# A graph attention kernel: three small products go from VectorE to GpSimd, weighted values one body later, score transposes to the middle of TensorE's body

## The chip, the cores and the metric

One core of a Trainium2 chip runs the whole program. The metric is the device time of one execution in microseconds, lower is better; the median of several executions is quoted. Five engines work side by side, each with its own instruction stream, and meet in semaphores: TensorE (PE), VectorE (DVE), ScalarE (ACT), GpSimd (POOL) and SyncE (SP, which only issues DMAs here).

## The reference, cut to what matters

A graph has N=6250 nodes and E=200000 edges, each edge with 128 features, a source `src` and a destination `dst`; the edges are sorted by `dst`. There are H=8 heads of D=16 values.

```python
ke = layer_norm(einsum('ef,hfd->hed', x_edge, Wke), gke, bke)   # ve likewise
rel_k = layer_norm(concatenate([ke, k[:, src]], -1) @ relk_W + relk_b, relk_g, relk_beta)
qk = sum(q[:, dst] * rel_k, -1) / 4.0                            # one score per edge and head
lse = log(segment_sum(exp(qk - m[dst]), dst)) + m                # m: maximum per node
rel_v = layer_norm(concatenate([ve, v[:, src]], -1) @ relv_W + relv_b, relv_g, relv_beta)
h = (qk - lse[dst])[..., None] * rel_v
agg = segment_sum(h, dst)
z = layer_norm(relu(agg @ z_W + z_b), z_g, z_beta)
x = layernorm(x + z)
```

Since `lse` is not known while the edges are walked, the kernel sums both `rel_v` and `qk * rel_v` per node and combines them at the end.

## The kernel before, in words

The program has three parts: `start` makes node tables and index data (some 200 us), `edges` walks the edges, and `tail` forms the log-sum-exp, combines the sums and writes the output (from about 2890 us on). The change touches `edges` alone.

**Tiling.** An edge group is 512 edges, four tiles of 128 (`GE`, `TILES`); there are `GROUPS` = 391. A batch is 3 groups. Every engine runs the same software pipeline: in its body `c` it does stage after stage, each on another group `x = c - lag`, so a body of an engine handles one group in each stage. `every` (L1001) writes 24 bodies out, puts 12 bodies in a hardware loop and writes the last ones out. The order of the stages in a body is written by hand, and so are the semaphore waits: each buffer is a ring indexed by `x` modulo its depth, and a stage waits for its inputs and for its ring slot to be free.

**A group's way** (in brackets the lag):
- SP loads the edge features (L1048, [0]), every third body the codes and the gather columns (L1064, L1065), the query rows (L1074, [1]), stores the sums (L1079, [12]) and every third body the transposed scores (L1091).
- PE transposes the features into the PSUM bank `eat_ps` (L1142, [0]); ACT copies them (L1213). PE projects them twice (`project`, L1120): for the layer norm's squares ([1]) and for the values ([3]). ACT squares (L1228), DVE reduces (L1420, [2]), ACT takes logarithm and exponential (L1235, L1249), DVE scales the values into `p` (L1402, [4]).
- POOL gathers the source nodes' rows by four indirect DMAs, one a tile (L1298, [3]), into a ring of three; it waits for the columns and for DVE's add of three groups before.
- DVE adds the rows to `p` (L1350, [5]). ACT squares it into `z` (L1221, [5]). PE makes 0/1 matrices from the codes (L1135 [4] and L1160 [5], both in the bank `misc`, copied by ACT in L1207 and L1242) and expands the queries (L1167, [5]). DVE multiplies queries by keys (L1367, [6]) and reduces squares and products to `zs` (L1385, [6]); ACT makes 1/norm for keys, `zr` (L1265, [7]), and for values, `zw` (L1266, [7]).
- Three DVE operations of 32 columns per partition follow, all [8]: the score's main part `qk0 = zs*zr` (L1358), the score `hh[.., 1, C] = qk0 + z[.., C]` (L1376), and the weight `zw[.., 1] = score * zw[.., 0]` (L1393). L1410 ([8]) multiplies the values by both weights into `hh`.
- PE sums `hh` by destination in two halves (`sums`, L1113, [9]), ACT copies each half (L1198).
- At a batch's end PE transposes its scores from `hh` into the bank `misc`, at the very end of the body (L1186, [9]), and ACT copies them at the end of its body (L1273). The next use of `misc` is L1135, at the start of PE's next body, which waits for that copy (`s_qktc`, L1134).

DVE's order in a body is L1350, L1358, L1367, L1376, L1385, L1393, L1402, L1410, L1420. PE's is L1135, L1142, first half of the sums, first projection, L1160, L1167, second half, second projection, L1186.

Of the kernel before, what the change touches and what calls it, by code (L numbers as in the profile page):

```python
# [5 lines left out]
P = 128  # L6
N, E, F, H, D = 6250, 200000, 128, 8, 16
C = D - 1
HC = H * C
TILES = 4  # L10
# [22 lines left out]
BATCH = 3  # L33
# [906 lines left out]
def edges(nc, a, t):  # L940
# [5 lines left out]
    EA, QR, RR, PR, HR, OR, AG, ZR = 4, 6, 3, 6, 6, 6, 4, 3  # L946
# [12 lines left out]
    zs = sb("e_zs", [P, 2, TILES, 3 * H])  # L959
    zln = sb("e_zln", [P, TILES, 2 * H])  # L960
    zr = sb("e_zr", [P, 2, TILES, H])
    zw = sb("e_zw", [P, 2, TILES, H, 2])
# [68 lines left out]
    with nc.Block(no_gpsimd_drain=True) as block:  # L1031
# [69 lines left out]
        def _(pe):  # L1101
# [22 lines left out]
            def body(c, i, loop):  # L1124
                x = c - 4
                if is_group(x, loop):
# [18 lines left out]
                x = c - 1  # L1145
                if is_group(x, loop):
# [4 lines left out]
                    project(x, i, 0, y_ps, s_y)  # L1151
                x = c - 5
                if is_group(x, loop):
                    n, k, kb = UNROLL * i + x, x % QR, (x // BATCH) % FB
                    pe.wait_ge(s_oht, n + 2 if loop or x < GROUPS - 1 else n + 1)
                    if not loop and x == GROUPS - 1:
                        pe.wait_ge(s_qktc, (x - 5 - (BATCH - 1)) // BATCH + 1)
# [12 lines left out]
                sums(c - 9, i, loop, 1)  # L1170
# [6 lines left out]
                x = c - 9  # L1177
                if is_batch_end(x, loop):
                    n, ng = UNROLL * i + x, groups_in(x, loop)
                    x0 = x - (ng - 1)  # L1180
                    pe.wait_ge(s_oh, n + 5 if loop or x + 5 <= GROUPS else GROUPS)
                    if loop or x >= BATCH:
                        pe.wait_ge(s_qktc, batch(x, i))
                    h0 = x0 % HR
                    src = hh[:, h0:h0 + ng, :, :, 1, C].rearrange("p g t h -> p (g t h)")
                    nc.tensor.transpose(misc[0:H * TILES * ng, 0:P], src, ident[:]).then_inc(s_qkt, 1)  # L1186
            every(pe, body, GROUPS + 9)

        @block.scalar
        def _(act):  # L1190
# [9 lines left out]
            def body(c, i, loop):  # L1200
# [13 lines left out]
                copy_sums(c - 9, i, loop, 0)  # L1214
# [22 lines left out]
                if is_group(x, loop):  # L1237
# [4 lines left out]
                    nc.scalar.activation(oh[:, x % OR, :, :].rearrange("p j n -> p (j n)"), misc, ACT.Relu).then_inc(s_oh, 1)  # L1242
                x = c - 3
# [7 lines left out]
                if is_group(x, loop):  # L1251
# [4 lines left out]
                    nc.scalar.activation(zln[:], zs[:, x % 2, :, 0:2 * H], ACT.Ln, bias=t["eps_c"][:, 0:1], scale=1.0 / D).then_inc(s_zl, 1)  # L1256
                copy_sums(c - 9, i, loop, 1)
                x = c - 7
                if is_group(x, loop):
                    n = UNROLL * i + x  # L1260
                    act.wait_ge(s_zl, n + 1)
                    if loop or x >= 2:
                        act.wait_ge(s_qk0, n - 1)
                        act.wait_ge(s_h, n - 1)
                    nc.scalar.activation(zr[:, x % 2, :, :], zln[:, :, 0:2 * H:2], ACT.Exp, scale=-0.5).then_inc(s_zr, 1)  # L1265
                    nc.scalar.activation(zw[:, x % 2, :, :, 0], zln[:, :, 1:2 * H:2], ACT.Exp, scale=-0.5).then_inc(s_zw, 1)  # L1266
                x = c - 9
                if is_batch_end(x, loop):
                    b, kb, ng = batch(x, i), (x // BATCH) % 2, groups_in(x, loop)
                    act.wait_ge(s_qkt, b + 1)  # L1270
                    if loop or x // BATCH >= 2:
                        act.wait_ge(s_qst[kb], 16 * (2 * i + (x // BATCH) // 2))
                    nc.scalar.activation(qkt[0:H * TILES * ng, kb, :], misc[0:H * TILES * ng, 0:P], ACT.Copy).then_inc(s_qktc, 1)  # L1273
            every(act, body, GROUPS + 9)

        @block.gpsimd
        def _(pool):
# [10 lines left out]
            def body(c, i, loop):  # L1288
                x = c - 3
                if is_group(x, loop):  # L1290
                    n, k, kb = UNROLL * i + x, x % RR, (x // BATCH) % FB
                    pool.wait_ge(s_ft[kb], 32 * (i + (x // BATCH) // FB + 1))
                    if loop or x >= RR:
                        pool.wait_ge(s_pt, n - RR + 1)
                    pool.reg_add(last_node, nodes_less_2, 1)
                    for j in range(TILES):
# [4 lines left out]
            every(pool, body, GROUPS + 3)  # L1301

        @block.vector
        def _(dve):
# [39 lines left out]
            def body(c, i, loop):  # L1344
# [7 lines left out]
                x = c - 8  # L1352
                if is_group(x, loop):
                    n = UNROLL * i + x
                    dve.wait_ge(s_zr, n + 1)
                    if loop or x >= 1:
                        dve.wait_ge(s_qk, n)
                    v.tensor_tensor(out=qk0[:], in0=zs[:, x % 2, :, 2 * H:3 * H], in1=zr[:, x % 2, :, 0:H], op=ALU.mult).then_inc(s_qk0, 1)  # L1358
# [10 lines left out]
                x = c - 8  # L1369
                if is_group(x, loop):  # L1370
                    n = UNROLL * i + x
                    dve.wait_ge(s_qk0, n + 1)
                    if loop or x >= HR:
                        dve.wait_ge(s_agg, 2 * (n - HR) + 2)
                        dve.wait_ge(s_qkt, batch(x - HR, i) + 1)
# [730 lines left out]
```

## Time and profile before

| | |
|---|---|
| median of 3 runs (lowest to highest) | 3233.97 us (3225.24 to 3234.28) |
| the profiled execution | 3227.16 us, span 3225.4 us |
| busy: DVE / PE / POOL / ACT | 93% / 89% / 77% / 72% of the span |
| DMA traffic | 722.70 MB, mean 224 GB/s |
| mean granted TensorE clock | 0.962, full in the loop |

The profile is of one execution. A row of the order of time gives start, duration (both us), engine, source line, operation, output <- input, the shapes, the count, and in square brackets how long the engine had been idle before and which engine's work ended that. Consecutive DVE operations overlap in the record: a duration holds about 0.08 us that run beside the next start, so the step from start to start is the cost in line. GpSimd's rows leave out the register instructions and waits between two DMAs.

### The profile page before, as it was taken

The page shows a single profiled execution, that of the slowest core. Times are in us where ns is not written, and L with a number is a line of the kernel's source. Part 1 is how long each engine was busy: PE and PEld are TensorE (multiplying, and loading weights), DVE is VectorE, ACT ScalarE, POOL GpSimd, SP SyncE. Part 2 cuts the span into 40 slices and gives each one's busy share as a digit, 9 for nine tenths or more (in the row PEclk, how much of TensorE's full clock was granted, in tenths as well). Part 3 has the DMA queues.
Part 4 walks back from the last instruction along what each step waited for, and adds up shares of the span by engine and source line. Part 5 has one row for each costly group of instructions (what it writes and reads, how often), then busy time and mean ns, then how long its engine had stood idle before and what let it go on. Part 6 is the DMA issues. An engine that isn't in the chain of part 4 may idle for free. (4 is left out here: it accounts for less than half of the span.)

```text
span 3225.4 us, 74832 instructions
## 1 busy us (share of the span) xinstructions
PE 2876.7 (89%) x18674; PEld 2508.7 (78%) x18870; DVE 3004.0 (93%) x4143; ACT 2333.4 (72%) x5276; POOL 2472.7 (77%) x1853
## 2 busy tenths in 40 slices
PE   4659999999999999999999999999999999975734
PEld 3348888888888888888888888888888888863523
DVE  7879999999999999999999999999999999975645
ACT  2448877888887888878888877888878788752425
POOL 6678888888888888888888888888888888843871
PEclk9889999999999999999999999999999999997966
DMA  4567888888888888888888888888888888856521
GB/s 90 153 178 236 251 251 248 248 246 249 249 250 248 248 246 250 249 251 249 247 246 249 249 250 248 248 246 250 249 248 249 246 248 249 256 187 144 168 54 42
DMA packets 660641, 722.70 MB, mean 224 GB/s; under 512 B 97970, under 2 KB 554279, under 8 KB 659934
## 3 DMA queue, kind: packets, MB, share of 16 engines
q1 hardware_dynamic: 568057, 505.84, 49.4%
q0 software_dynamic: 84896, 211.67, 25.0%
q10 hardware_dynamic: 7620, 4.43, 0.6%
q8 instruction: 25, 0.41, 0.0%
q14 instruction: 43, 0.34, 0.0%
HBM read 482.87 MB, written 237.97 MB: 223 GB/s over the span
## 5 line engine op out<-in xcount | busy, mean ns | idle before, releaser
L1298 POOL DMA_INDIRECT e_rows<-node_table,e_gcol x1564 | 2181.0, 1395 | 479.0 <-issue 476.9
L1120 PE MATMUL banks<-w_edge,e_eat 128*128 128x240 f32 x6256 | 1399.2, 367 | 3.2 <-DVE e_p L1402 2.6
L1120 PEld LDWEIGHTS banks<-w_edge,e_eat 128*128 128x128 f32 x6256 | 1179.6, 190 | 115.4 <-DVE e_p L1402 11.3
L1113 PE MATMUL banks<-e_h,e_oh 128*128 128x256 f32 x3128 | 826.2, 387 | 8.2 <-ACT e_agg L1198 4.2
L1385 DVE TENSOR_REDUCE e_zs<-e_z 128x96 f32<-128x1440 f32 x391 | 646.2, 1653 | 0.2
L1113 PEld LDWEIGHTS banks<-e_h,e_oh 128*128 128x128 f32 x3128 | 533.5, 190 | 52.2 <-DVE e_h L1410 5.1
L1198 ACT ACTIVATE e_agg<-banks 128x512 f32<-128x512 f32 x782 | 465.4, 595 | 104.2 <-PE banks L1113 103.9
L1402 DVE TENSOR_TENSOR e_p<-banks,e_yr 128x960 f32<-128x960 f32 x391 | 449.1, 1149 | 3.4 <-PE banks L1120 3.4
L1410 DVE TENSOR_TENSOR e_h<-e_p,e_zw 128x960 f32<-128x960 f32 x391 | 449.3, 1149 | 0.1
L1350 DVE TENSOR_TENSOR e_p<-e_p,e_rows 128x960 f32<-128x960 f32 x391 | 449.3, 1149 | 0.0
L1420 DVE TENSOR_REDUCE e_yvar<-e_ysq 128x64 f32<-128x960 f32 x391 | 448.3, 1147 | 0.0
L1207 ACT ACTIVATE e_oht<-banks 128x512 bf16<-128x512 f32 x391 | 233.5, 597 | 282.6 <-remote 143.2
L1228 ACT ACTIVATE e_ysq<-banks 128x960 f32<-128x960 f32 x391 | 379.8, 971 | 50.4 <-PE banks L1120 6.7
L1221 ACT ACTIVATE e_z<-e_p 128x960 f32<-128x960 f32 x391 | 390.1, 998 | 0.0
L1167 PE MATMUL banks<-e_q,e_oht 128*128 128x128 bf16 x4692 | 325.8, 219 | 1.3 <-DVE e_z L1367 1.3
L1142 PE MATMUL banks<-ident,e_ea 128*128 128x128 f32 x1564 | 236.8, 274 | 77.5 <-ACT e_qkt L1273 43.1
L1167 PEld LDWEIGHTS banks<-e_q,e_oht 128*128 128x128 bf16 x4692 | 278.3, 98 | 1.7 <-issue 1.6
L1367 DVE TENSOR_TENSOR e_z<-e_p,banks 128x512 f32<-128x512 f32 x391 | 266.2, 681 | 0.0
L1142 PEld LDWEIGHTS banks<-ident,e_ea 128*128 128x128 f32 x1564 | 193.1, 141 | 80.3 <-DMA e_ea<-in_edge_attr 29.1
L1213 ACT ACTIVATE e_eat<-banks 128x512 f32<-128x512 f32 x391 | 231.2, 591 | 22.7 <-PE banks L1142 22.6
L1242 ACT ACTIVATE e_oh<-banks 128x512 f32<-128x512 f32 x391 | 229.6, 587 | 0.0
L1160 PEld LDWEIGHTS banks<-rank_code,e_feat 128*128 128x128 bf16 x1564 | 120.0, 98 | 46.1 <-ACT e_oht L1207 0.5
(412 smaller groups left out, 2570.6 us busy)
## 6 DMA issues: line engine op xcount, KB each, us to landing
tile_sums<-e_agg SPq DMA_DIRECT2D x391, 512.0 KB
e_q<-q_by_rank SPq DMA_DIRECT2D x1564, 96.0 KB
e_ea<-in_edge_attr SPq DMA_DIRECT2D x390, 256.0 KB
e_rows<-node_table,e_gcol POOLq DMA_INDIRECT x1564
edge_lse<-t_lse_sb SPq DMA_DIRECT2D x14, 448.0 KB, 3.6
edge_qk<-e_qkt SPq DMA_DIRECT2D x130, 48.0 KB
node_table<-n_tb SPq DMA_DIRECT2D x24, 240.0 KB, 2.6
t_x<-edge_qk SPq DMA_DIRECT2D x2, 2240.0 KB
```

Source lines behind the costliest of these rows:

```text
L1113: last = nc.tensor.matmul(agg_ps[:, (j % 2) * AW:(j % 2 + 1) * AW], oh[:, x % OR, j, :], hh[:, x % HR, j, :, :, :].rearrange("p h s d -> p ...
L1120: last = nc.tensor.matmul(out_ps[:, j // 2, (j % 2) * 2 * HC:(j % 2 + 1) * 2 * HC], eat[:, x % 4, j * P:(j + 1) * P], t["w_edge"][:, at:at ...
L1142: last = nc.tensor.transpose(eat_ps[:, j * P:(j + 1) * P], ea[:, k, j, :], ident[:])
L1167: last = nc.tensor.matmul(qx_ps[:, j * F:(j + 1) * F], oht[:, x % 2, j * P:(j + 1) * P], qw[:, k, j, part * F:(part + 1) * F], start=(part ...
L1198: nc.scalar.activation(agg[:, k, 2 * half:2 * half + 2, :].rearrange("p j c -> p (j c)"), agg_ps, ACT.Copy).then_inc(s_ags, 1)
L1221: nc.scalar.activation(z[:, x % ZR, :, 0:2 * H, 0:C], p[:, k, :, :, :, 0:C].rearrange("p t h k c -> p t (h k) c"), ACT.Square).then_inc(s_ ...
L1298: g.indirect_dma_start(out=rows[:, k, j, :], out_offset=None, in_=table, in_offset=bass.IndirectOffsetOnAxis(ap=gcol[:, kb, at:at + 1].bit ...
L1350: v.tensor_tensor(out=p[:, k, :, :, :, 0:C].rearrange("p t h k c -> p (t h k) c"), in0=p[:, k, :, :, :, 0:C].rearrange("p t h k c -> p (t ...
L1385: v.tensor_reduce(out=zs[:, x % 2, :, :], in_=z[:, x % ZR, :, :, 0:C], axis=AX.X, op=ALU.add).then_inc(s_z, 1)
L1402: v.tensor_tensor(out=p[:, k, :, :, :, 0:C].rearrange("p (b t) h k c -> p b (t h k) c", b=2), in0=u_ps.rearrange("p b (h c) -> p b h c", c=C),
L1410: v.tensor_tensor(out=hh[:, x % HR, :, :, :, 0:C].rearrange("p t h s c -> p (t h) s c"), in0=p[:, k, :, :, 1, 0:C].rearrange("p t h c -> p ...
L1420: v.tensor_reduce(out=yvar[:, x % 2, :, :], in_=ysq[:, x % 2, :, :].rearrange("p t (h c) -> p t h c", c=C), axis=AX.X, op=ALU.add).then_in ...
```

## The change

What it does:
- POOL takes over the three operations of 32 columns ([8] in its own body). In a body it issues two of the four gathers, then `qk0` and the score, then the other two gathers, then the weight. The second product waits for the first, the first for `zr` from ACT.
- DVE does L1410 for a group one body later ([9]); the sums of PE and the copies of ACT follow ([10] for [9]). The rings of `zs`, `zr`, `zw` grow from 2 to 4.
- PE transposes the scores in the middle of its body, after the first projection, for lag [10], into `eat_ps`; it waits for POOL's scores and for ACT's copy of the current features. L1142 waits for the copy of the scores (`s_qktc`) where L1135 did. ACT copies the scores between L1242 and L1249.
- SP is not edited; its store of the scores keeps its place and its wait for `s_qktc`.

The diff, cut to its core:

```diff
-    EA, QR, RR, PR, HR, OR, AG, ZR = 4, 6, 3, 6, 6, 6, 4, 3
+    EA, QR, RR, PR, HR, OR, AG, ZR, WR = 4, 6, 3, 6, 6, 6, 4, 3, 4
...
-    zs = sb("e_zs", [P, 2, TILES, 3 * H])
+    zs = sb("e_zs", [P, WR, TILES, 3 * H])
...
@@ tensor
-                    if loop or x >= 6 + BATCH - 1:
-                        pe.wait_ge(s_qktc, batch(x - 6 - (BATCH - 1), i) + 1)
                     nc.tensor.matmul(misc, t["nfeat"][:], feat[:, kb, (x % BATCH) * GE:(x % BATCH + 1) * GE], start=True, stop=True).then_inc(s_ohtp, 1)
...
+                    if loop or c >= 11 + BATCH - 1:
+                        pe.wait_ge(s_qktc, batch(c - 11 - (BATCH - 1), i) + 1)
                     for j in range(TILES):
                         last = nc.tensor.transpose(eat_ps[:, j * P:(j + 1) * P], ea[:, k, j, :], ident[:])
                     last.then_inc(s_tr, 1)
-                sums(c - 9, i, loop, 0)
+                sums(c - 10, i, loop, 0)
...
                     project(x, i, 0, y_ps, s_y)
+                x = c - 10
+                if is_batch_end(x, loop):
+                    n, ng = UNROLL * i + x, groups_in(x, loop)
+                    x0 = x - (ng - 1)
+                    pe.wait_ge(s_qk, n + 1)
+                    pe.wait_ge(s_eat, UNROLL * i + c + 1 if is_group(c, loop) else GROUPS)
+                    if loop or x >= BATCH:
+                        pe.wait_ge(s_qktc, batch(x, i))
+                    h0 = x0 % HR
+                    src = hh[:, h0:h0 + ng, :, :, 1, C].rearrange("p g t h -> p (g t h)")
+                    nc.tensor.transpose(eat_ps[0:H * TILES * ng, 0:P], src, ident[:]).then_inc(s_qkt, 1)
...
@@ gpsimd
+            def gathers(x, i, loop, first):
...
+                    for j in (first, first + 1):
...
+            def body(c, i, loop):
+                gathers(c - 3, i, loop, 0)
+                x = c - 8
...
+                    pool.wait_ge(s_zr, n + 1)
+                    if loop or x >= 1:
+                        pool.wait_ge(s_qk, n)
+                    g.tensor_tensor(out=qk0[:], in0=zs[:, x % WR, :, 2 * H:3 * H], in1=zr[:, x % WR, :, 0:H], op=ALU.mult).then_inc(s_qk0, 1)
...
+                    pool.wait_ge(s_qk0, n + 1)
+                    if loop or x >= HR:
+                        pool.wait_ge(s_agg, 2 * (n - HR) + 2)
+                        pool.wait_ge(s_qkt, batch(x - HR, i) + 1)
+                    g.tensor_tensor(out=hh[:, x % HR, :, :, 1, C], in0=qk0[:], in1=z[:, x % ZR, :, 2 * H:3 * H, C], op=ALU.add).then_inc(s_qk, 1)
+                gathers(c - 3, i, loop, 2)
...
+                    pool.wait_ge(s_qk, n + 1)
+                    pool.wait_ge(s_zw, n + 1)
+                    if loop or x >= WR:
+                        pool.wait_ge(s_h, n - WR + 1)
+                    g.tensor_tensor(out=zw[:, x % WR, :, :, 1], in0=hh[:, x % HR, :, :, 1, C], in1=zw[:, x % WR, :, :, 0], op=ALU.mult).then_inc(s_w2, 1)
...
@@ vector
-                    v.tensor_tensor(out=qk0[:], in0=zs[:, x % 2, :, 2 * H:3 * H], in1=zr[:, x % 2, :, 0:H], op=ALU.mult).then_inc(s_qk0, 1)
...
-                    v.tensor_tensor(out=hh[:, x % HR, :, :, 1, C], in0=qk0[:], in1=z[:, x % ZR, :, 2 * H:3 * H, C], op=ALU.add).then_inc(s_qk, 1)
...
-                    v.tensor_tensor(out=zw[:, x % 2, :, :, 1], in0=hh[:, x % HR, :, :, 1, C], in1=zw[:, x % 2, :, :, 0], op=ALU.mult).then_inc(s_w2, 1)
...
-                x = c - 8
+                x = c - 9
                 if is_group(x, loop):
                     n, k = UNROLL * i + x, x % PR
                     dve.wait_ge(s_w2, n + 1)
 ...
```

## Rows read from the trace of the kernel before

**Rows 1.** Busy time in the loop; columns: window, PE, PEld, DVE, ACT, POOL, clock, DMA.
```profile
1000.00:1500.00 500.00, 485.71 (x3299) 434.89 (x3334) 500.00 (x661) 401.87 (x906) 410.29 (x295) 1.00 0.82 248
```

**Rows 2.** In order of time, DVE, one body from L1410 to L1410.
```profile
1505.99 1.15 DVE L1410 TENSOR_TENSOR e_h<-e_p,e_zw 128x960 f32<-128x960 f32 x1
...
1508.12 1.15 DVE L1350 TENSOR_TENSOR e_p<-e_p,e_rows 128x960 f32<-128x960 f32 x1
1509.19 0.19 DVE L1358 TENSOR_TENSOR e_qk<-e_zs,e_zr 128x32 f32<-128x32 f32 x1
1509.29 0.68 DVE L1367 TENSOR_TENSOR e_z<-e_p,banks 128x512 f32<-128x512 f32 x1
1509.88 0.21 DVE L1376 TENSOR_TENSOR e_h<-e_qk,e_z 128x32 f32<-128x32 f32 x1
1510.06 1.65 DVE L1385 TENSOR_REDUCE e_zs<-e_z 128x96 f32<-128x1440 f32 x1
1511.63 0.20 DVE L1393 TENSOR_TENSOR e_zw<-e_h,e_zw 128x32 f32<-128x32 f32 x1
1511.75 1.15 DVE L1402 TENSOR_TENSOR e_p<-banks,e_yr 128x960 f32<-128x960 f32 x1
1512.81 1.15 DVE L1410 TENSOR_TENSOR e_h<-e_p,e_zw 128x960 f32<-128x960 f32 x1
```

**Rows 3.** In order of time, DVE, the last add of L1350.
```profile
2869.23 1.16 DVE L1350 TENSOR_TENSOR e_p<-e_p,e_rows 128x960 f32<-128x960 f32 x1
```

**Rows 4.** In order of time, PE, a batch's end and the body after it.
```profile
1507.87 0.27 PE L1186 MATMUL banks<-ident,e_h 128*96 128x128 f32 x1
1508.61 0.39 PE L1135 MATMUL banks<-e_feat,rank_code 128*128 128x512 bf16 x1 [0.46 <-ACT e_qkt L1273]
1508.83 0.60 PE L1142 MATMUL banks<-ident,e_ea 128*128 128x128 f32 x4
...
1515.40 0.60 PE L1142 MATMUL banks<-ident,e_ea 128*128 128x128 f32 x4
```

**Rows 5.** In order of time, DVE, first bodies, before L1410 and the small operations run.
```profile
228.01 1.15 DVE L1350 TENSOR_TENSOR e_p<-e_p,e_rows 128x960 f32<-128x960 f32 x1
229.07 0.68 DVE L1367 TENSOR_TENSOR e_z<-e_p,banks 128x512 f32<-128x512 f32 x1
229.86 1.65 DVE L1385 TENSOR_REDUCE e_zs<-e_z 128x96 f32<-128x1440 f32 x1
...
233.55 1.15 DVE L1350 TENSOR_TENSOR e_p<-e_p,e_rows 128x960 f32<-128x960 f32 x1
```

**Rows 6.** In order of time, POOL, beside rows 2.
```profile
1506.29 1.74 POOL L1298 DMA_INDIRECT e_rows<-node_table,e_gcol  x1 [0.30 <-issue]
1508.34 1.82 POOL L1298 DMA_INDIRECT e_rows<-node_table,e_gcol  x1 [0.30 <-issue]
1510.46 1.02 POOL L1298 DMA_INDIRECT e_rows<-node_table,e_gcol  x1 [0.30 <-issue]
```

**Rows 7.** One line's instructions, L1298: duration ns min/median/max, first and last start.
```profile
L1298 POOL DMA_INDIRECT e_rows<-node_table,e_gcol x1564: 1015/1029/1832, 203.2 to 2860.1; - x196
```

**Rows 8.** In order of time, POOL, beside rows 5.
```profile
234.33 1.26 POOL L1298 DMA_INDIRECT e_rows<-node_table,e_gcol  x1 [0.30 <-issue]
```

**Rows 9.** In order of time, POOL, products in the tail.
```profile
3140.10 1.27 POOL L1548 TENSOR_TENSOR t_fresh<-t_fresh,t_beta_b 128x512 f32<-128x512 f32 x1
...
3166.15 0.59 POOL L1548 TENSOR_TENSOR t_fresh<-t_fresh,t_beta_b 106x128 f32<-106x128 f32 x1 [6.93 <-DMA t_fresh<-in_x]
```

**Rows 10.** In order of time, DVE, beside rows 9.
```profile
3140.12 1.81 DVE L1769 TENSOR_TENSOR t_x<-t_sums,t_x 128x512 f32<-128x512 f32 x1
...
3161.96 0.68 DVE L1769 TENSOR_TENSOR t_x<-t_sums,t_x 128x512 f32<-128x512 f32 x1
...
3165.75 0.68 DVE L1721 TENSOR_TENSOR t_x<-t_x,in_chunk 128x512 f32<-128x512 f32 x1
```

**Rows 11.** In order of time, ACT, beside rows 2.
```profile
1507.09 0.23 ACT L1265 ACTIVATE e_zr<-e_zln 128x32 f32<-128x32 f32 x1
```

More of the change, by code:

```diff
@@ L1169, in body @@
                     last.then_inc(s_qx, 1)
-                sums(c - 9, i, loop, 1)
+                sums(c - 10, i, loop, 1)
                 x = c - 3
@@ L1176, in body @@
                     project(x, i, 2 * HC, u_ps, s_u)
[L1177 to L1187, printed above, removed]
+            every(pe, body, GROUPS + 10)
         @block.scalar
@@ L1213, in body @@
                     nc.scalar.activation(eat[:, c % 4, :], eat_ps, ACT.Copy).then_inc(s_eat, 1)
-                copy_sums(c - 9, i, loop, 0)
+                copy_sums(c - 10, i, loop, 0)
                 x = c - 5
@@ L1242, in body @@
                     nc.scalar.activation(oh[:, x % OR, :, :].rearrange("p j n -> p (j n)"), misc, ACT.Relu).then_inc(s_oh, 1)
+                x = c - 10
+                if is_batch_end(x, loop):
+                    b, kb, ng = batch(x, i), (x // BATCH) % 2, groups_in(x, loop)
+                    act.wait_ge(s_qkt, b + 1)
+                    if loop or x // BATCH >= 2:
+                        act.wait_ge(s_qst[kb], 16 * (2 * i + (x // BATCH) // 2))
+                    nc.scalar.activation(qkt[0:H * TILES * ng, kb, :], eat_ps[0:H * TILES * ng, 0:P], ACT.Copy).then_inc(s_qktc, 1)
                 x = c - 3
@@ L1261, in body @@
                     act.wait_ge(s_zl, n + 1)
[L1262 to L1274, printed above, removed]
+                    if loop or x >= WR:
+                        act.wait_ge(s_qk0, n - WR + 1)
+                        act.wait_ge(s_h, n - WR + 1)
+                    nc.scalar.activation(zr[:, x % WR, :, :], zln[:, :, 0:2 * H:2], ACT.Exp, scale=-0.5).then_inc(s_zr, 1)
+                    nc.scalar.activation(zw[:, x % WR, :, :, 0], zln[:, :, 1:2 * H:2], ACT.Exp, scale=-0.5).then_inc(s_zw, 1)
+            every(act, body, GROUPS + 10)
         @block.gpsimd
@@ L1286, in _ @@
             nodes_less_2 = pool.to_reg(N - 2)
-            def body(c, i, loop):
-                x = c - 3
+            def gathers(x, i, loop, first):
                 if is_group(x, loop):
                     n, k, kb = UNROLL * i + x, x % RR, (x // BATCH) % FB
-                    pool.wait_ge(s_ft[kb], 32 * (i + (x // BATCH) // FB + 1))
-                    if loop or x >= RR:
-                        pool.wait_ge(s_pt, n - RR + 1)
+                    if first == 0:
+                        pool.wait_ge(s_ft[kb], 32 * (i + (x // BATCH) // FB + 1))
+                        if loop or x >= RR:
+                            pool.wait_ge(s_pt, n - RR + 1)
                     pool.reg_add(last_node, nodes_less_2, 1)
-                    for j in range(TILES):
+                    for j in (first, first + 1):
                         at = (x % BATCH) * TILES + j
@@ L1420, in body @@
                     v.tensor_reduce(out=yvar[:, x % 2, :, :], in_=ysq[:, x % 2, :, :].rearrange("p t (h c) -> p t h c", c=C), axis=AX.X, op=ALU.add).then_inc(s_yv, 1)
-            every(dve, body, GROUPS + 8)
+            every(dve, body, GROUPS + 9)
     ph.close([])
```

51 lines of the change are left out of this document (19 added, 32 removed).

## The prediction

> **What bounds the kernel now.** I read the busy time of a stretch of the loop first, then one body on each engine, in order of time, then the few places where POOL and DVE meet. In 500 us of the loop [rows 1] DVE is busy for all of them, PE for 486, ACT for 402, POOL for 410, with the clock granted in full: look for the engine whose busy time equals the stretch. [Rows 2] are DVE's body; the step from one start to the next is the price of an operation in line. They follow each other with no gap: 1.07 (L1350), 0.10 (L1358), 0.59 (L1367), 0.18 (L1376), 1.57 (L1385), 0.12 (L1393), 1.06 (L1402) and 2.13 for L1410 and L1420 make 6.82 with rounding. The last of the 391 adds of L1350 stands at 2869.23 [rows 3], the fourth at 233.55 [rows 5], so 387 bodies took 6.81 us each: DVE's own sum is the kernel's period.
>
> PE is close behind. Its body runs from one start of L1142 to the next: 6.57 us from 1508.83 to 1515.40 [rows 4], and every third body is longer, because the score transpose (1507.87) is followed by a wait for its copy until 1508.61, 0.74 us. (3x6.57+0.74)/3 is 6.82: with DVE's 6.81 these two are level. So taking DVE's small operations away alone would gain nothing: PE needs 6.8 as well. The change touches both.
>
> POOL looks free (82%), but is not simply so. Unhindered, a gather takes 1.02 us (the shortest and the median of all are 1015 and 1029 ns [rows 7]) and 0.30 lies between two, so four take 5.28. In each body two take 1.74 and 1.82 instead: the one that starts inside L1410's time, and the one that starts inside L1350's [rows 2, 6]. The 1506.29 gather ends at 1508.03, 0.89 after L1410 has ended at 1507.14; the 1508.34 one ends at 1510.16, 0.89 after L1350 has ended at 1509.27. The other two of a body start beside L1385 and L1402 and take 1.02. So a gather's start has to wait out a DVE operation whose two inputs both lie in SBUF. 5.28+0.72+0.80=6.80 is DVE's body: POOL has no other idle time and is held in step by these blocks. They are elastic: before L1410 had begun to run, DVE's body was 5.54 (228.01 to 233.55 [rows 5]), and the block was 0.24 (the gather of 1.26 [rows 8]): 5.28+0.24=5.52.
>
> **DVE's part.** Removed are L1358 and L1393, 0.10+0.12. L1376 (0.18) frees nothing: it now hides the end of L1367, on which L1385 depends. Where nothing lay between them, in the first bodies, L1385 started 0.79 after L1367 [rows 5], against 0.59+0.18=0.77 now. Gain 0.22-0.02, less what rounding hides: 0.20 to 0.22, I take 0.21; new sum 6.60 (by the early body: 5.54 and 1.06 for L1410). L1410 one body later changes what it reads, not its price; its input from POOL has a whole body more to arrive.
>
> **PE's part.** The wait of 0.74 goes; the transpose moves between the first projection and L1160, writes the bank of the edge transposes, and its copy by ACT has until the next body's L1142. Its wait for that bank's earlier copy is over before (a whole group of sums and a projection lie between), and PE's wait for the copy, now ahead of L1142, comes a second projection later. The copy itself moves ahead of ACT's L1249, whose result DVE's L1402 needs; it holds it up by 0.27 in each third body, and as ACT is free for a fifth of its time [rows 1] I count nothing; uncovered it would be 0.09 per body. The transpose itself I bound by nothing and by its recorded 0.27 [rows 4]: 6.57 to 6.66 per body, and take 0.11, since four of the same shape in L1142 take 0.44 until the next group: 6.61. SP stores both scores and sums twelve groups behind, and they are now there at ten instead of nine; the loads queued behind those stores are made a body or more ahead of their use, so nothing; with that lead gone PE would wait for edge features ahead of L1142.
>
> **POOL's part.** Three products of 32 columns. No row has this shape. One of 512 columns took 1.27; the one of 128 columns took 0.59, of which 0.17 was waiting for L1721 (3165.75 to 3166.44, let go 0.12 before its recorded end, as gathers are: 1507.14-1506.29-0.12 is 0.73), so 0.42 [rows 9, 10]. The line through both has 2.2 ns per column and 0.14 at none: 0.21 us for 32 columns. Bounds: 0.14 (no column costs anything) and 0.42 (the 128-column one). With one wait of a product for the one before (0.18, as DVE's own in [rows 5]: 0.79 for L1367 against 0.59 to 0.60), POOL's unhindered body is 5.28+3x0.21+0.18=6.09; at the bounds 5.88 and 6.72. At 6.09 it fits into 6.61 if it is blocked for no more than 0.52 per body, where it is blocked for 1.52 today. I take it that it fits, because the block shrank to 0.24 in [rows 5, 8] when DVE's body shrank: POOL slips until the blocks fill what is left. The new wait for ACT's s_zr holds the two later gathers and all behind them; L1265 has it at 1507.32 [rows 11], before the second gather (by count from the first, that of 1506.29) ends at 1508.03. DVE's waits are on products half a body to a body old, L1410's on one made a body before. The gathers have lead: POOL's last began at 2860.1 [rows 7], its add at 2869.23, 9 us later.
>
> **The sum.** DVE 6.60, PE 6.61, POOL within; two engines so close pass 0.01 of waits to each other: 6.62. 6.81-6.62, taken unrounded as 0.195, by 385 full bodies is 75 us. The last group goes through one body more and through three POOL operations: 2 us back. So 73: 3227.2 of the profiled execution becomes 3154, and since that one lies 7 below the median of the runs shown, the median 3234 becomes 3161; I say 3160. A change of 0.3% (10 us) is about what a measurement can tell from none.
>
> [...] The trace shows both directions: gathers blocked by DVE [rows 2, 6], and DVE's L1769, 0.68 alone, taking 1.81 while a POOL product ran from 3140.10 to 3141.37 [rows 9, 10]. [...]
>
> **The rivals.** *POOL becomes the bound* (the one on the slower side). The place is POOL's body, the price 6.09 plus the blocks. It decides when products and blocks do not fit into 6.61, from 0.52 of blocks on, or a product over about 0.35. With one whole block (0.80) left it is 6.89, 0.08 more than now: 385x0.08+2 is 33, so 3267. With both of today's it is 7.61: 3544. Then DVE would wait in L1367 for the second product. For it: seven starts per body can be caught where there were four, and at 0.42 a product POOL's sum alone is over. Against it: the elasticity above, and 0.21 being well under the limit.
>
> *DVE is blocked by the products.* L1350 or L1410 wait behind a product that has just started, 0.21-0.12=0.09 each time. One such wait per body: 6.71, gain 0.10x385-2, 3197. With all three in the way, 6.89, which is the first rival's price again. For it: L1769. Against it: a POOL that is held in step starts its operations as DVE's end, not just ahead of them.
>
> *The gain is not there* (PE's 6.57 hides a wait that takes the place of the transpose's): then PE's mean stays at 6.8, and 3234 is the time. Against it: two bodies in three already run in 6.57.
>
> **The chances.** Forecast 0.67 (3146 to 3178, the upper end being PE's 6.66: 385x0.15-2 is 56); DVE blocked in part 0.10; no gain 0.05; POOL the bound 0.18. The range reaches from DVE's 6.60 (gain 0.21x385, less 2, with a run 7 under the median) at 3146 to 3205, just above the case of DVE blocked in part, and leaves out the last two cases. Faster 0.77, same 0.05, slower 0.18.
>
> **What would show it.** Right: L1350 to L1350 in 6.60 to 6.63 with L1385 0.78 behind L1367; no 0.74 gap ahead of L1135, PE's body 6.57 and 6.68 in every third; POOL's products at about 0.21, and fewer and shorter gathers over 1.02. Wrong: DVE idle ahead of L1367 for a POOL product, with a period of 6.9 or more; L1350 or L1410 longer than 1.15; products of 0.4; PE idle ahead of L1142 for the copy of the scores.

## The result and the profile after

The kernel after takes 3326.9 us (median of 4 runs, 3321.24 to 3330.66) where the kernel before takes 3229.6 beside it (4 runs): a ratio of 1.030, 95% interval 1.027 to 1.033. The prediction, 3160 with a range of 3146 to 3205, is wrong, and on the wrong side. The first rival, POOL becomes the bound, named the place; a second loss, a stall of ACT once per pass of the loop, stood in no case. The profiled execution has a span of 3328.8 us.

Busy time in the same stretch as [rows 1], same columns:

```profile
1000.00:1500.00 500.00, 479.36 (x3191) 422.13 (x3191) 470.55 (x424) 380.98 (x870) 414.85 (x494) 0.99 0.81 239
```

No engine fills the stretch any more: DVE 471 where it had 500, PE 479 where it had 486, POOL 415. So each of them waits for a part of it. The waits from 1000 to 2500 us of the kernel after (engine, line, engine and line waited for: us in total, times, longest):

```profile
ACT e_agg L1197 <- issue: 63.7, 21, 3.9
PEld banks L1113 <- ACT e_agg L1197: 55.0, 21, 3.4
ACT e_oht L1206 <- issue: 54.2, 19, 3.8
DVE e_z L1387 <- POOL e_h L1318: 51.9, 202, 0.3
...
POOL e_h L1318 <- POOL e_qk L1310: 49.0, 207, 0.3
```

There are two patterns. One is in nearly every body (202 times in 1500 us): DVE's product of queries and keys (L1387, before L1367) waits 0.26 us for POOL's second product (L1318). The other comes some 20 times on each of two ACT lines, about once per line in each of the 17.6 passes of the 12-body loop, and is long: ACT stands for up to 3.9 us and waits for nothing the profile can name ("issue"), and PE then waits for ACT.

**The steady body.** In order of time, first POOL, then DVE, beside [rows 2, 6]:

```profile
1505.48 0.27 POOL L1310 TENSOR_TENSOR e_qk<-e_zs,e_zr 128x32 f32<-128x32 f32 x1
1505.98 0.92 POOL L1318 TENSOR_TENSOR e_h<-e_qk,e_z 128x32 f32<-128x32 f32 x1 [0.24 <-POOL e_qk L1310]
1507.05 1.04 POOL L1298 DMA_INDIRECT e_rows<-node_table,e_gcol  x1
1508.39 1.02 POOL L1298 DMA_INDIRECT e_rows<-node_table,e_gcol  x1 [0.31 <-issue]
1509.44 0.29 POOL L1327 TENSOR_TENSOR e_zw<-e_h,e_zw 128x32 f32<-128x32 f32 x1
1509.89 1.04 POOL L1298 DMA_INDIRECT e_rows<-node_table,e_gcol  x1 [0.16 <-issue]
1511.24 1.25 POOL L1298 DMA_INDIRECT e_rows<-node_table,e_gcol  x1 [0.30 <-issue]
1512.51 0.26 POOL L1310 TENSOR_TENSOR e_qk<-e_zs,e_zr 128x32 f32<-128x32 f32 x1
```

```profile
1505.55 1.22 DVE L1377 TENSOR_TENSOR e_p<-e_p,e_rows 128x960 f32<-128x960 f32 x1
1507.04 0.69 DVE L1387 TENSOR_TENSOR e_z<-e_p,banks 128x512 f32<-128x512 f32 x1 [0.27 <-POOL e_h L1318]
1507.82 1.65 DVE L1397 TENSOR_REDUCE e_zs<-e_z 128x96 f32<-128x1440 f32 x1
1509.39 1.15 DVE L1406 TENSOR_TENSOR e_p<-banks,e_yr 128x960 f32<-128x960 f32 x1
...
1512.58 1.21 DVE L1377 TENSOR_TENSOR e_p<-e_p,e_rows 128x960 f32<-128x960 f32 x1
```

Read the two fences against each other. POOL's first product starts at 1505.48 and is done at 1505.75. DVE's add L1377 (before L1350) is recorded from 1505.55, and finishes 0.07 late. The second product depends on the first and starts only at 1505.98; L1377, with both inputs in SBUF, is then running, and the product takes 0.92 us where the undisturbed one takes 0.27. DVE's next operation, L1387, writes a slot of the three-deep ring of `z` that this very product reads, so it may start only at 1507.04: 1.49 us from L1377 to L1387 where a DVE in step needs 1.07 [rows 2]. The body is 6.60+0.42=7.02 us (1512.58-1505.55 is 7.03). It is a closed circle: DVE's add delays the product, the product delays DVE's next operation, and so the add meets the product again in the next body.

**The stall.** ACT in order of time, around the start of one pass; the two idle stretches come in every pass:

```profile
933.23 0.60 ACT L1206 ACTIVATE e_oht<-banks 128x512 bf16<-128x512 f32 x1 [2.62 <-issue]
...
937.08 0.60 ACT L1197 ACTIVATE e_agg<-banks 128x512 f32<-128x512 f32 x1 [2.77 <-issue]
```

and the instruction queue on the page of the kernel after, then of the kernel before:

```profile
q14 instruction: 187, 1.52, 0.1%
```

```profile
q14 instruction: 43, 0.34, 0.0%
```

So 144 more packets of instructions were fetched, 1.18 MB or 8 KB each. They lie inside the loop, about five per pass: from 1000 to 2500 us the queue has 89 in the kernel after and none in the kernel before. Of ACT's "issue" waits of over 0.6 us in the loop, 58 of 60 have a packet starting inside them.

### The profile page after: what moved, and what is told of

Same layout as the page of the kernel before. It is cut to its first block and busy times, and to the rows that moved or that the text cites. A ratio compares the mean times of both kernels' runs of the same rounds, so it can differ in the third digit from the quotient of the medians.

```text
span 3328.8 us, 75925 instructions
## 1 busy us (share of the span) xinstructions
PE 2954.2 (89%) x18870; PEld 2537.9 (76%) x18870; DVE 2944.7 (88%) x2970; ACT 2313.3 (69%) x5276; POOL 2588.9 (78%) x3026
## 3 DMA queue, kind: packets, MB, share of 16 engines
q14 instruction: 187, 1.52, 0.1%
## 5 line engine op out<-in xcount | busy, mean ns | idle before, releaser
L1298 POOL DMA_INDIRECT e_rows<-node_table,e_gcol x1564 | 1722.9, 1102 | 371.3 <-issue 316.4
L1120 PE MATMUL banks<-w_edge,e_eat 128*128 128x240 f32 x6256 | 1432.9, 373 | 19.7 <-DVE e_p L1406 16.6
L1120 PEld LDWEIGHTS banks<-w_edge,e_eat 128*128 128x128 f32 x6256 | 1196.3, 193 | 172.3 <-DVE e_p L1406 71.8
L1113 PE MATMUL banks<-e_h,e_oh 128*128 128x256 f32 x3128 | 849.4, 395 | 89.5 <-ACT e_agg L1197 87.0
L1397 DVE TENSOR_REDUCE e_zs<-e_z 128x96 f32<-128x1440 f32 x391 | 646.2, 1653 | 40.2 <-DVE e_z L1387 7.8
L1113 PEld LDWEIGHTS banks<-e_h,e_oh 128*128 128x128 f32 x3128 | 543.7, 194 | 144.0 <-ACT e_agg L1197 91.9
L1197 ACT ACTIVATE e_agg<-banks 128x512 f32<-128x512 f32 x782 | 464.6, 594 | 202.2 <-PE banks L1113 101.6
L1206 ACT ACTIVATE e_oht<-banks 128x512 bf16<-128x512 f32 x391 | 233.4, 597 | 420.5 <-PE banks L1133 334.4
L1377 DVE TENSOR_TENSOR e_p<-e_p,e_rows 128x960 f32<-128x960 f32 x391 | 469.9, 1202 | 16.8 <-DMA e_rows<-node_table,e_gcol 14.5
L1414 DVE TENSOR_TENSOR e_h<-e_p,e_zw 128x960 f32<-128x960 f32 x391 | 449.8, 1151 | 5.7 <-POOL e_zw L1327 5.7
L1318 POOL TENSOR_TENSOR e_h<-e_qk,e_z 128x32 f32<-128x32 f32 x391 | 346.0, 885 | 87.7 <-POOL e_qk L1310 83.8
L1387 DVE TENSOR_TENSOR e_z<-e_p,banks 128x512 f32<-128x512 f32 x391 | 268.5, 687 | 91.0 <-POOL e_h L1318 90.7
L1142 PEld LDWEIGHTS banks<-ident,e_ea 128*128 128x128 f32 x1564 | 195.8, 141 | 101.9 <-DMA e_ea<-in_edge_attr 32.2
L1142 PE MATMUL banks<-ident,e_ea 128*128 128x128 f32 x1564 | 236.1, 274 | 30.4 <-DMA e_ea<-in_edge_attr 30.4
```

What stands on the lines that cost most here:

```text
L1113: last = nc.tensor.matmul(agg_ps[:, (j % 2) * AW:(j % 2 + 1) * AW], oh[:, x % OR, j, :], hh[:, x % HR, j, :, :, :].rearrange("p h s d -> p ...
L1120: last = nc.tensor.matmul(out_ps[:, j // 2, (j % 2) * 2 * HC:(j % 2 + 1) * 2 * HC], eat[:, x % 4, j * P:(j + 1) * P], t["w_edge"][:, at:at ...
L1197: nc.scalar.activation(agg[:, k, 2 * half:2 * half + 2, :].rearrange("p j c -> p (j c)"), agg_ps, ACT.Copy).then_inc(s_ags, 1)
L1298: g.indirect_dma_start(out=rows[:, k, j, :], out_offset=None, in_=table, in_offset=bass.IndirectOffsetOnAxis(ap=gcol[:, kb, at:at + 1].bit ...
L1377: v.tensor_tensor(out=p[:, k, :, :, :, 0:C].rearrange("p t h k c -> p (t h k) c"), in0=p[:, k, :, :, :, 0:C].rearrange("p t h k c -> p (t ...
L1397: v.tensor_reduce(out=zs[:, x % WR, :, :], in_=z[:, x % ZR, :, :, 0:C], axis=AX.X, op=ALU.add).then_inc(s_z, 1)
```

## The experiments

Theory A: the body of 7.02 us comes from POOL's second product standing right behind the first. Theory B: the stall of ACT is a loss of its own. The recorded expectations use these letters for their own pairs of theories. `e1`, `e2` and `e4` ran beside the kernel before at 3227.05 us.

**Products back on DVE** (`e1_products_on_dve`): the three products leave POOL and stand in DVE's body at their old places; all else of the change stays.

```diff
 # pool
                 gathers(c - 3, i, loop, 0)
-                (qk0, score for x = c - 8)
                 gathers(c - 3, i, loop, 2)
-                (weight for x = c - 8)
 # vector: the three, [8], where L1358, L1376, L1393 stood
+                v.tensor_tensor(out=qk0[:], ...); v.tensor_tensor(out=hh[..., 1, C], ...); v.tensor_tensor(out=zw[..., 1], ...)
```

> The changed kernel with its three small products given back to DVE (at their old places in DVE's body); the lag of one body for L1410 and the sums, and the early score transpose on PE, stay. Theory A (POOL's products alone make the loss): DVE's sum is the old 6.81 us per body, PE's 6.61 is hidden under it, so the time is that of the kernel before, 3225 to 3235 us, and PE shows no gap of 0.74 ahead of the code matmul. Theory B (PE's new order or the longer lag loses time as well, by a wait or by instruction fetches in the loop): 3250 or more. The stall of ACT of some 2.8 us once in every pass of the 12-body loop, worth some 28 us, stays by B and goes by A.

3298.78 us, 1.022 (1.020 to 1.024). Ten of twelve bodies take 6.8 us, the DVE sum of before, one per pass takes 7.0 and one 8.1 to 9.6. The page again shows 187 packets, and the waits show

```profile
ACT e_agg L1197 <- issue: 52.9, 19, 3.7
```

The 7.02 us bodies are gone with POOL's products; the stall is not. Two losses, then: theory B of this run, 3250 or more with the stall left, came true.

**Score transpose back at the end of the body** (`e2_transpose_at_end`): POOL keeps its products; PE's transpose and ACT's copy go back to the bank `misc` at the end of their bodies.

```diff
 # tensor, middle of the body
-                    nc.tensor.transpose(eat_ps[0:H * TILES * ng, 0:P], src, ident[:]).then_inc(s_qkt, 1)
 # tensor, end of the body
+                    nc.tensor.transpose(misc[0:H * TILES * ng, 0:P], src, ident[:]).then_inc(s_qkt, 1)
 # scalar: the copy of it likewise to the end of the body; s_qktc is waited for ahead of L1133 again
```

> The changed kernel with the score transpose and its copy back at the ends of PE's and ACT's bodies, in the old bank; products stay on POOL. Theory A (POOL's body of 7.02 us is the bound): PE's 6.81 is hidden under 7.02, 3320 to 3335 us, no difference from the changed kernel. Theory B (the place of the transpose costs or helps now): more than 10 us either way.

3347.15 us, 1.035 (1.032 to 1.039), 20 us above the kernel after and outside the 3320 to 3335 of theory A. So the early transpose is worth something even where other waits hide much of it. The wait it removes is there again:

```profile
ACT e_qkt L1274 <- PE banks L1187: 54.2, 64, 2.1
PEld banks L1135 <- ACT e_qkt L1274: 53.6, 70, 1.1
```

**Products spread** (`e4_spread`): one gather between any two of POOL's products.

```diff
-                gathers 0, 1;  qk0;  score;  gathers 2, 3;  weight
+                gather 0;  qk0;  gather 1;  score;  gather 2;  weight;  gather 3
```

> The changed kernel with POOL's order gather, first product, gather, second product, gather, third product, gather. The second product no longer stands right behind the first, on which it depends, so no DVE operation can slip in between, and its wait lies beside a gather. Theory A (the pair in a row, 0.24 us of wait and 0.65 of block, is what makes 7.02 of 6.27): the pair's wait goes, POOL's unhindered sum is about 6.0, period 6.62 to 6.75, 3165 to 3215 us. Theory D (three more starts per body are too many wherever they stand): 6.95 or more, 3300 to 3400.

3283.65 us, 1.016 (1.012 to 1.019), between the ranges of both theories. About a third of the bodies take 6.59 to 6.63 us where the kernel after has 7.02, but the longest of each pass takes 7.2 to 10.2 us, and many take 6.9 to 7.8. That the stall covers the gain of theory A is, here, only a guess; `e10_spread_moved_act` below tests it.

**A first attempt to move ACT's loop, which moved nothing.** If the stall is a matter of where ACT's loop lies in its instruction stream, instructions ahead of the loop must move it. A first set put additions to a register there (24 for three kernels, 119 for the kernel before), with these expectations. Theory F in them takes up what the kernel after shows: 144 more packets of 8 KB, ACT's waits of 3.0 us on average at L1197 (63.7 in 21) and of 2.9 at L1206 (54.2 in 19), and a loop of 318 instructions with its branch:

> The changed kernel with 24 register additions put ahead of ACT's loop and nothing else. Theory F (the change shifted the place of ACT's 318-instruction loop in its instruction stream, so that it is fetched anew in every pass, 144 more packets of 8 KB on the instruction queue and a stall of 2 to 3.5 us per pass): the fetches in the loop go, bodies stay at 7.02 us because POOL is the bound, 3295 to 3312 us. Rival G (the stalls belong to the changed order of waits, not to the place of the code): 3321 to 3331 us as before the padding. Rival H (without the stalls POOL keeps its lead): 6.6 per body, 3155 to 3180.

> The kernel with POOL's products spread between its gathers (run before at 3284 us, its bodies 6.60 us between the stalls), with the same 24 register additions on ACT. Theory F: no stall per pass, all bodies 6.60 to 6.63 us, 3155 to 3180 us. Rival G: 3270 to 3288 us. Rival D (POOL is the bound in the long run even so): 3200 to 3260.

> [...] Theory F with blocks of 8 KB: one longer body of some 9 us in every pass as in the run with the products on DVE, about 2.3 us times 30, 3290 to 3305 us, and some 5 instruction packets in every pass. If the block is 16 KB, or the place of the code is not the cause: 3225 to 3237.

> The changed kernel with its products given back to DVE (3299 us), with 24 register additions on ACT. Theory F: 11 of 12 bodies there took 6.82 and one 9.0 to 9.3; that one becomes 6.82 as well, 3222 to 3235 us. Rival G: 3298 to 3306 us.

The additions are not among the executed instructions: ACT ran 10957 (kernel before: 10989) with and without them. So these four are repeats of the kernel after, of `e4_spread`, of the kernel before and of `e1_products_on_dve`, and none of their theories was tested. They ran on another chip, on which the kernel before took 3466.8 us, 7% more, and gave 3448.44 (0.993), 3380.81 (0.977), 3477.57 (1.005, interval 1.002 to 1.007, of the kernel before against itself) and 3547.82 (1.025). The interval of that third ratio leaves out 1 for one and the same program, so a difference of 0.5% is not safe here. There ACT's copies of the sums also wait 188 us in 1500 in the kernel before for something the profile calls "remote"; by the code that is the store of an earlier group's sums. Most bodies of the kernel before take 6.8 to 7.6 us, a few up to 9, and the ranking is another: the kernel after is the faster one by 0.7%. The fetches are as on the first chip, 186 or 187 packets in three of them and 42 in the kernel before. I draw no more from this chip than that a change that costs 3% in one place may gain 0.7% in another. What differs, the chip or its state at the time, no run shows.

**ACT's loop really moved.** Real instructions do it: activations of one column, in a stretch in which ACT is idle (21.3 us in the kernel before, up to 203.38). The next four kernels ran beside the kernel before at 3228.05 us.

```diff
         @block.scalar
         def _(act):
+            for k in range(24):                  # 119 in e12
+                nc.scalar.activation(pad[:, k:k + 1], t["eps_c"][:], ACT.Copy)
```

By the records of the trace, counted from 0, ACT's loop begins with instruction 704 in the kernel before and with 695 in the kernel after. With its branch it is 319 long before and 318 after. With 24 more it begins with 719, and the kernel before with 119 more begins it with 823.

> The kernel after with the three products on DVE, and 24 activations of one column put ahead of ACT's loop, in a stretch in which ACT is idle, so that ACT's loop lies 24 instructions further on in its stream. Theory F (once per pass of the loop ACT waits for a piece of its own instructions, because of where its loop lies in them; the kernel before has none of it): the 144 further packets of the instruction queue are gone, every body takes 6.8 us, the pass 82 us, and the time falls by the stall of 2.4 us in each of 30 passes, to 0.98 of the same kernel without the 24 (3299 us on a chip where the kernel before takes 3227), within 0.5% of the kernel before. Rival (the stall comes from the length or the order of the changed loops, not from the place): the stall stays, and the time is 1.02 of the kernel before.

3236.61 us, 1.002 (1.001 to 1.004); 10 runs. Every pass takes 82.0 us, where without the 24 instructions it took 84.1 on average. The page:

```profile
q14 instruction: 42, 0.34, 0.0%
```

The stall was worth 62 us here (3299 to 3237). What is left of the change, PE's part and the later L1414, gains nothing with DVE's sum at 6.82; the prediction had said the same of the other half ("taking DVE's small operations away alone would gain nothing"). It costs 9 us by medians, which the times alone hardly tell from nothing, but the trace has a place for most of it: one body per pass takes 7.01 us, so a pass takes 81.97 where the kernel before has 81.79. Why that one is longer is open; `e10` and `e13` have one of 6.76 per pass.

> The kernel after with POOL's products spread between all four gathers, and 24 activations of one column ahead of ACT's loop. Theory F with theory A (the body of 7.02 us comes from the two neighbouring products of POOL, and the rest from the stall of ACT): no instruction packets in the loop, bodies of 6.60 us, a pass of 79.4 us, and 0.975 to 0.98 of the kernel before (3150 to 3165 us where that takes 3227). If the place has nothing to do with the stall: 1.015, as without the 24.

3159.5 us, 0.979 (0.976 to 0.981), as expected, and the fastest kernel of this study. The stretch, then POOL and DVE in order of time:

```profile
1000.00:1500.00 500.00, 500.00 (x3417) 444.44 (x3416) 492.27 (x454) 409.11 (x931) 435.13 (x528) 1.00 0.86 255
```

```profile
1507.58 0.26 POOL L1314 TENSOR_TENSOR e_qk<-e_zs,e_zr 128x32 f32<-128x32 f32 x1
1508.00 1.04 POOL L1302 DMA_INDIRECT e_rows<-node_table,e_gcol  x1 [0.16 <-POOL e_qk L1314]
1509.07 0.28 POOL L1323 TENSOR_TENSOR e_h<-e_qk,e_z 128x32 f32<-128x32 f32 x1
...
1510.59 0.72 POOL L1332 TENSOR_TENSOR e_zw<-e_h,e_zw 128x32 f32<-128x32 f32 x1
...
1512.80 1.38 POOL L1302 DMA_INDIRECT e_rows<-node_table,e_gcol  x1 [0.30 <-issue]
```

```profile
1505.52 1.14 DVE L1383 TENSOR_TENSOR e_p<-e_p,e_rows 128x960 f32<-128x960 f32 x1
...
1508.92 1.15 DVE L1412 TENSOR_TENSOR e_p<-banks,e_yr 128x960 f32<-128x960 f32 x1
1509.99 1.18 DVE L1420 TENSOR_TENSOR e_h<-e_p,e_zw 128x960 f32<-128x960 f32 x1
...
1512.15 1.14 DVE L1383 TENSOR_TENSOR e_p<-e_p,e_rows 128x960 f32<-128x960 f32 x1
```

PE is now the full engine, with 6.63 us per body. The score's product (1509.07) runs beside L1412, which takes one of its inputs from PSUM, takes 0.28 us, and is done 3.9 us ahead of the L1393 that needs it (1513.21). POOL is blocked twice, by 0.44 (L1332, beside L1420) and 0.36 (1512.80): 0.80 us of blocks in a body of 6.62, and they delay nobody. Without them POOL's body is 5.82, which is 0.34 less than in the kernel after (6.16, worked out below), because fewer idle gaps lie between its operations.

> The kernel after, with only the 24 activations ahead of ACT's loop. Theory F and A together: the stall goes, bodies of 7.02 us stay, a pass is 84.2 us and the kernel 1.01 to 1.025 of the kernel before: the body's own loss is shown alone. If the stall was what threw POOL out of the faster order: bodies of 6.61 us and 0.98. If the place has nothing to do with the stall: 1.03 as before.

3317.27 us, 1.027 (1.024 to 1.030), just above the 1.01 to 1.025 expected: the loss of the body alone. The fetches are gone (41 packets), every pass takes 84.4 us, and the waits keep only the first pattern:

```profile
DVE e_z L1391 <- POOL e_h L1322: 55.3, 214, 0.3
...
POOL e_h L1322 <- POOL e_qk L1314: 50.6, 214, 0.3
```

So by medians the stall costs only 10 us of the 97 in the kernel after. In the profiled executions a pass of the kernel after takes 85.2 us on average against 84.4, and the stretch from DVE's first add to its last is 22 us longer; the parts before and after it took 11 us more in `e11`. Either way it is less than the 62 with the products on DVE: a DVE that waits 0.42 in every body has slack with which it catches up (behind a body of 8.21 us stand 6.73 and 6.59). And the stall was not what brought the slow order about.

> The kernel before, with 119 activations of one column ahead of ACT's loop, so that it lies as the loop of the kernel after would lie against pieces of 128 instructions. Theory F: packets of the instruction queue appear in the loop, one body per pass grows by 2 to 3 us, and the kernel takes 1.015 to 1.025 of the kernel before. If the place has nothing to do with the stall: the same time within 0.5% (the 119 take about 0.2 us each, in a stretch where ACT is idle for 20 us, so a few us at most).

3340.96 us, 1.034 (1.031 to 1.037), more than the 1.015 to 1.025 expected: the kernel before, with all its old work in its old order, loses 113 us by 119 small instructions that run once. Some 9 us of that are their own time: they take 11.2 us (200.97 to 212.19), longer than was left of the idle stretch, and ACT's first copy of features starts at 212.09 instead of 203.38. The rest, some 104 us, comes from inside the loop, where one body per pass takes 9.3 to 11.5 us. The page, and ACT in order of time in one pass:

```profile
q14 instruction: 188, 1.54, 0.1%
```

```profile
1543.70 0.27 ACT L1277 ACTIVATE e_qkt<-banks 96x128 f32<-96x128 f32 x1 [0.82 <-PE banks L1187]
1548.30 0.60 ACT L1211 ACTIVATE e_oht<-banks 128x512 bf16<-128x512 f32 x1 [4.33 <-issue]
...
1550.22 0.60 ACT L1202 ACTIVATE e_agg<-banks 128x512 f32<-128x512 f32 x1 [0.82 <-issue]
```

Here the last operation of ACT's pass is followed by nothing for 4.33 us, as the loop starts again. DVE then waits 2.80 us for ACT's `zr`. The place is thereby shown both ways: moving the loop away from the place of the kernel after removes the fetches and the stall in three kernels, and moving the kernel before to a bad place brings them.

**First product earlier** (`e13_first_product_first`, with the 24 instructions; kernel before 3226.46): is it the gap between two dependent products, or did the single gathers help?

```diff
+                qk0
                 gathers 0, 1
-                qk0;  score
+                score
                 gathers 2, 3;  weight
```

> The kernel after with the 24 activations ahead of ACT's loop, and with POOL's first product put ahead of the first pair of gathers, one place earlier: the gathers stay in pairs, and the second product, where it was, no longer stands right behind the one it depends on. Theory A (the loss is the 0.24 us gap between two dependent products, into which DVE's add slips, and not the number of products or their load on POOL): bodies of 6.60 to 6.70 us, no wait of DVE's product of the score for POOL's second product, 0.978 to 0.985 of the kernel before (3155 to 3180 us where that takes 3227). Rival (it was the single gathers between the products that helped, by giving each product a place behind a DVE operation): bodies near 7.0 us and 1.02 to 1.03.

3178.62 us, 0.985 (0.983 to 0.987), bodies of 6.66 to 6.69 us from the fifth on, but for one of 6.76 per pass. One product moved by one place turns 3317 into 3179. In order of time, POOL, then DVE:

```profile
1506.43 0.72 POOL L1322 TENSOR_TENSOR e_h<-e_qk,e_z 128x32 f32<-128x32 f32 x1
...
1508.65 1.39 POOL L1302 DMA_INDIRECT e_rows<-node_table,e_gcol  x1 [0.30 <-issue]
```

```profile
1505.80 1.23 DVE L1418 TENSOR_TENSOR e_h<-e_p,e_zw 128x960 f32<-128x960 f32 x1
...
1509.08 0.68 DVE L1391 TENSOR_TENSOR e_z<-e_p,banks 128x512 f32<-128x512 f32 x1
```

The score's product is still blocked (0.72 against 0.27), but by L1418 instead of the add L1381, two operations earlier in DVE's order, and it is ready 1.9 us before L1391. So a blocked product alone costs nothing: what cost in the kernel after is a block right in front of the operation that waits for the product. One thing is not separated: here too POOL's own body is shorter, 6.68 less blocks of 0.45 and 0.37 is 5.86, against 6.16. No run has POOL's longer sum with the product in a harmless place, or the shorter sum with the product in the bad one. The last 0.05 to 0.07 us against `e10_spread_moved_act` are L1418, 1.23 us where it takes 1.15 elsewhere; what lengthens it I did not settle.

A fourth slot in the ring of `z` would let L1387 go ahead without the product and would test the circle directly. `e3_z_ring_4` was written for it, with 3270 to 3390 us expected if POOL's own body bounds and 3160 to 3200 if the ring is the cause. It has no result: the four slots do not fit into SBUF (16384 bytes per partition are needed for the sums' buffer, 11872 are left). So that test stays open.

## Why the prediction was wrong, step by step

- **DVE's part, right.** L1397 follows L1387 by 0.78 us (1507.04 to 1507.82), 0.77 to 0.79 predicted; where DVE waits for nobody its body is 6.59 to 6.63, against 6.60.
- **PE's part, right.** The 0.74 gap is gone. In `e10_spread_moved_act` the plain body takes 6.61 (1505.45 to 1512.06) and that with the transpose 6.68 (1512.06 to 1518.74), the transpose itself 0.12 (1514.98 to 1515.10), against 6.57, 6.68 and 0.11. The mean is 6.63, against 6.61.
- **POOL's sum, a little low.** The products take 0.26 to 0.29 instead of 0.21, and 0.24 lies between dependent ones instead of 0.18; only 0.15 to 0.16, instead of a gather's 0.30, lies behind a product. From the body shown above, 7.03 less the blocks of 0.65 (second product) and 0.22 (the gather of 1.25) leaves 6.16 unhindered, against 6.09. That alone would still have fit if the blocks had shrunk to 0.45.
- **"I take it that it fits": the step that failed.** I let POOL slip until its blocks fill what is left, because nobody was taken to wait for POOL. But L1387 does, on a slot of `z`, once per body: it waits 0.27 us, the body takes 7.02 instead of 6.62, and the blocks are 0.87 instead of the 0.52 that I had allowed. I had written that DVE's waits are on "products half a body to a body old"; that holds for the first bodies, and then the lead is eaten up. The distance from the end of the score's product to L1387, from the order of time of the kernel after, is 4.9 to 5.1 us for the first seven products, then 3.7 and 3.2, then 1.6 or 1.4 for eight more, and 0.1 from the eighteenth on. The forecast's own order, bodies of 6.61 to 6.62 us, is there for bodies 5 to 9 and is not held. It was possible and not stable: nothing pushed POOL back. The first thing that differs is a gather at 273.28 that started 0.32 us late (0.75 idle before it, 0.43 in the bodies before). The gathers behind it (274.62 and 276.85) then ran into L1414 and L1377. That this late start drove the order off is the likely reading, not a tested one:

```profile
272.25 0.27 POOL L1318 TENSOR_TENSOR e_h<-e_qk,e_z 128x32 f32<-128x32 f32 x1
273.28 1.03 POOL L1298 DMA_INDIRECT e_rows<-node_table,e_gcol  x1 [0.75 <-issue]
274.62 1.76 POOL L1298 DMA_INDIRECT e_rows<-node_table,e_gcol  x1 [0.30 <-issue]
...
276.85 1.78 POOL L1298 DMA_INDIRECT e_rows<-node_table,e_gcol  x1 [0.16 <-issue]
```

  Why it was late is open; the same late gather and the same dent (a body of 6.73 or 6.74) are there in `e11_after_moved_act`. In `e10_spread_moved_act` no gather of these bodies starts late; after its longer bodies (6.76, one per pass) the next is 6.6 again.
- **The first rival, right in place, and near in price.** It had DVE waiting in L1367 for the second product, and it happens. It gave 6.89 for one whole block and 7.61 for two; with the measured blocks of 0.87 its sum gives 6.96, and measured is 7.02. It took the blocks for a load on POOL, though, and left out that DVE's wait brings the block back in every body. Its threshold of 0.52 holds only for POOL's sum of 6.09: `e10_spread_moved_act` carries 0.80 of blocks in 6.62, with a sum of 5.82. `e13_first_product_first` shows the rest: which operation is blocked, and who waits for it, matters too.
- **The second rival, true and small.** L1377 takes 1.22 beside the product, 0.07 more, where 0.09 was estimated; it is part of the 0.42.
- **ACT, not in the text at all.** In the kernel after nine instructions fewer stand ahead of ACT's loop, and that changes the loop's place. A bad place costs 10 us by medians in the kernel after, 62 with the products on DVE, some 104 in the kernel before, and 124 with the products spread (3284 to 3160 by medians).
- **The lower end of the range.** 0.21x385 less 2 and less 7 is 86 off 3234, so 3148; the 3146 leaves the 2 out. Nothing hangs on it.

Together: from the 3159.5 us of the order that works, the circle of product and ring costs 158 (3317), and the stall 10 more (3327). The forecast of 3160 is met by a kernel that the change is not: that `e10_spread_moved_act` lands on it confirms the sums for DVE and PE, not the step on POOL.

What the traces show of the two causes. POOL's second product takes 0.92 us in the kernel after, where it starts while DVE's L1377 runs, and 0.72 in `e13_first_product_first`, beside L1418; both of these DVE operations have two inputs in SBUF. It takes 0.27 undisturbed, and 0.28 beside L1412, which has one input in PSUM. In the kernel with 119 more instructions ACT records no operation for 4.33 us as its loop starts again, and an 8 KB packet of the instruction queue starts within that time, at 1546.60. Of the beginnings of the loop four were run: at 695 and 823 it is fetched again, at 704 and 719 it is not. 695 and 823 lie 128 apart, so they lie alike in pieces of 128 instructions, which `e12_before_moved_act` assumed, and 704 and 719 lie otherwise. That fits, but how many instructions a packet holds, and how much of a loop is kept from pass to pass, no run shows. `e7_before_act_pad` set blocks of 8 KB against blocks of 16: the packets have 8 KB on q14 (1.52 MB in 187 in the kernel after) and 16 on q8 (0.43 MB in 26), but as its loop did not move it tests neither. All this rests on the trace recording every instruction ahead of the loop.

## What to carry to other kernels

When work moves to an engine that is held up while another's operations run (here 0.92 us for a product of 0.27), its sum and its blocks are not enough: for each moved operation look up who waits for it and which operation of the other engine it will run beside. Keep an independent instruction between two dependent small ones, and the consumer's wait far from the block: here one product moved by one place turned 3317 us into 3179. When every pass of a loop is slower by the same few us with "issue" waits on one engine, compare the packets of the instruction queue before blaming the work (here 187 against 43), and try a few instructions ahead of the loop (here 24, 3284 to 3160 us).

## What the runs showed that I had not expected

- The place of a loop in an engine's instruction stream can be worth over 3%: 3228 to 3341 us by 119 instructions that do no work (some 9 us of it their own time), 3284 to 3160 by 24. The loop was not fetched again when it began with instruction 704 or 719, and was when it began with 695 or 823.
- A POOL product of 128x32 takes 0.26 to 0.29 us, with 0.15 behind it up to the next instruction, and 0.24 (in early bodies 0.08) up to one that depends on it.
- Two engines that block each other, here by a POOL product that takes 0.92 us instead of 0.27 while DVE's add runs, and by a ring on which DVE waits 0.27, can run the same work in 6.62 or 7.02 us per body. One and the same kernel held the faster order for five bodies, and left it after a gather that came 0.32 us late.
- Another chip ran the same program 7% slower at a fully granted clock (1.00 from 1000 to 1500 us), with 188 us of "remote" waits ahead of ACT's copies of the sums, and there the change made it faster (0.993, 0.990 to 0.997).
